# VectorE's row products put into loops with register addresses, in a BatchNorm convolution gate over two images

## The reference, cut to what matters

```python
xg  = group_norm(x, 32 groups)                       # no affine
y1  = bn_relu(sum over h of xg[b,c,h,:] * w1[c,h])   # (b, c, 256)
y2  = bn_relu(sum over w of xg[b,c,:,w] * w2[c,w])   # (b, c, 256)
dot = sum over k of y1[b,c,k] * y2[b,c,k]
p   = softmax over c of ((dot @ lw1.T + lb1) @ lw2.T + lb2)
out = x + xg * p[b,c]
```

## Time and profile before

| What | Value |
|---|---|
| Median of three runs | 1724.97 us |
| The profiled execution, its own time | 1723.45 us |
| Its span on the core | 1721.1 us |
| DMA, moved over the span | 724.02 MB, mean 421 GB/s |
| VectorE busy | 928.2 us, 54% |
| ScalarE busy | 664.3 us, 39% |
| TensorE busy (matmuls) | 561.4 us, 33% |
| GpSimd busy | 336.8 us, 20% |
| VectorE's row products (L920) | 1856, busy 643.1 us, with 155.0 us of accumulator reads |

### The profile page before, as it was taken

One profiled execution on the slowest core, in us unless ns is written; L12 is line 12 of the kernel. 1 busy time (PEld: TensorE's weight loads), 2 busy tenths in 40 slices (PEclk: granted clock), 3 DMA queues, 4 the chain that ended last, 5 costly groups with the idle time before them and its releaser, 6 DMA issues.

```text
span 1721.1 us, 14879 instructions
## 1 busy us (share of the span) xinstructions
PE 561.4 (33%) x4326; PEld 229.5 (13%) x4326; DVE 928.2 (54%) x4104; ACT 664.3 (39%) x507; POOL 336.8 (20%) x475
## 2 busy tenths in 40 slices
PE   4588766554334433433354344430000000000000
PEld 1123212122111211111121122110000000000000
DVE  5899999957455655555566547772222222222220
ACT  4687987856344455444555446610000000000000
POOL 7678888820000000000000000000000000000000
PEclk8799888876565655656556555765555555555555
DMA  9999999989999999999999999989999999999999
GB/s 394 425 427 426 415 396 425 429 342 419 430 429 429 431 430 430 429 431 429 430 430 430 401 429 430 401 331 431 433 432 428 431 433 432 432 429 431 433 432 404
DMA packets 52146, 724.02 MB, mean 421 GB/s; under 512 B 6241, under 2 KB 6753, under 8 KB 8034
## 3 DMA queue, kind: packets, MB, share of 16 engines
q1 hardware_dynamic: 33922, 458.84, 62.9%
q10 hardware_dynamic: 18144, 264.25, 36.1%
HBM read 454.63 MB, written 268.44 MB: 420 GB/s over the span
## 4 chain that ended last, share of the span: by engine, by line
DMA 51%; another core or an unknown queue 27%; DVE 7%; PE 6%; ACT 3%; issue 2%; SPq 1%; POOL 0%; ACTq 0%; DVEq 0%; POOLq 0%
DMA xs<-in_x 44%; DMA out<-xs 6%; DVE mul_junk L920 5%; PE ps_part L521 2%; ACT sq_junk L733 2%; DVE xs L994 2%; DMA xs<-in_w 1%; SPq L344 1%; ACT xs L800 1%; PE ps_part L651 1%; PE ps_part L536 1%; PE ps_y L549 1%; PE ps_l L613 0%; PE ps_l L622 0%
## 5 line engine op out<-in xcount | busy, mean ns | idle before, releaser
L920 DVE SCALAR_TENSOR_TENSOR mul_junk<-xs,ps_w 128x256 fp8e5<-128x256 f32 x1856 | 643.1, 418 | 291.4 <-DMA xs<-in_x 288.7
L733 ACT ACTIVATE sq_junk<-xs 128x4096 fp8e5<-128x4096 f32 x128 | 463.3, 3619 | 284.5 <-DMA xs<-in_x 276.1
L994 DVE TENSOR_SCALAR xs<-xs,scale,shift 128x4096 f32<-128x4096 f32 x95 | 227.1, 2412 | 392.0 <-DMA xs<-in_x 391.4
L536 PE MATMUL ps_part<-xs,taps 128*32 128x256 f32 x2048 | 221.7, 609 | 414.4 <-DMA xs<-in_x 414.4
L521 PE MATMUL ps_part<-xs,taps 128*32 128x512 f32 x1024 | 157.8, 764 | 104.5 <-DMA xs<-in_x 99.8
L800 ACT ACTIVATE xs<-xs,shift,scale 128x4096 f32<-128x4096 f32 x33 | 125.4, 3801 | 112.2 <-DMA xs<-in_x 107.9
L536 PEld LDWEIGHTS ps_part<-xs,taps 128*32 128x32 f32 x2048 | 92.9, 163 | 522.7 <-issue 350.1
L434 POOL TENSOR_TENSOR rstd_b<-var,minus_half 128x1 f32<-128x1 f32 (+1 forms) x36 | 20.5, 568 | 708.7 <-DVE var L944 708.7
L920 DVE DVE_READ_ACCUMULATOR mul_junk<-xs,ps_w 128x1 f32 x1856 | 155.0, 83 | 0.0
L405 POOL TENSOR_TENSOR xs<-xs 128x768 f32<-128x768 f32 x64 | 116.4, 1824 | 59.6 <-DMA xs<-in_x 56.8
L521 PEld LDWEIGHTS ps_part<-xs,taps 128*32 128x32 f32 x1024 | 44.2, 135 | 208.2 <-issue 208.2
(11 more groups left out here) (108 smaller groups left out, 348.2 us busy)
## 6 DMA issues: line engine op xcount, KB each, us to landing
xs<-in_x SPq DMA_DIRECT2D x214, 2048.0 KB, 27.6
out<-xs ACTq DMA_DIRECT2D x126, 2048.0 KB, 33.3
xs<-in_lw SPq DMA_DIRECT2D x2, 2048.0 KB, 16.0
out<-xs SPq DMA_DIRECT2D x2, 2048.0 KB, 11.1
w_c<-in_w_rows SPq DMA_DIRECT2D x1, 512.0 KB, 3.8
w_sb<-in_w SPq DMA_DIRECT2D x1, 512.0 KB, 9.0
xs<-in_w SPq DMA_DIRECT2D x1, 512.0 KB, 23.2
xs<-in_g SPq DMA_DIRECT2D x2, 16.0 KB
```

The lines of the kernel that those rows point to most:

```text
L536: last = nc.tensor.matmul(ps_part[b][32 * a:32 * a + 32, 0:W], taps[:, g % 2, hf * JH + j, :], xs[:, s, j * W:(j + 1) * W], start=(hf == 0 ...
L733: nc.scalar.activation(sq_junk[:], xs[:, s, :], ACT.Square, accum_out=sq_sum[:, u % 2, u // 2, b:b + 1], saturate=False).then_inc(squared, 1)
L920: last = nc.vector.scalar_tensor_tensor(out=mul_junk[:, sets[0] % 2, j - first, :], in0=xs[:, s, j * W:(j + 1) * W], scalar=1.0, saturate= ...
L994: return nc.vector.tensor_scalar(xs[:, s, :], xs[:, s, :], scale[:, b, g:g + 1], shift[:, b, g:g + 1], ALU.mult, ALU.add)
```

## The change

`multiply_rows` no longer writes its rows out: each half-unit's sets become a loop on VectorE, whose counter gives the addresses of the row in `xs`, of the column in `y2s` and, in the first stage, of the scratch row. The loop's counter also gives the value that `rows_done` must have.

In the first stage the loop runs over three sets, and the thirteenth row stands behind it. Each of the 13 rows has a scratch row of its own (`early_junk`, uint8, in the part of slot 9 that the first stage uses for small things); a set waits for the same set of the half-unit before. In the second stage the loop runs over four sets, all write to the same four rows of `mul_junk` (now bf16, without a second buffer), and each set waits for the one right before it. `rows_done` starts at `SETS` instead of 0, and the waits on it on SyncE and TensorE are raised by as much.

```diff
+def rows_before(u, b):
+    return SETS * (position(u, b) + 1)
...
+        early_junk = early(DVE_ROWS * W // 4).bitcast(mybir.dt.uint8).rearrange("p (r w) -> p r w", r=DVE_ROWS)
...
-        mul_junk = sb("mul_junk", [P, 2, SET, W], mybir.dt.float8e5)
+        mul_junk = sb("mul_junk", [P, SET, W], bf16)
...
-                sp.wait_ge(rows_done, SETS * (position(u, b) + 1))
+                sp.wait_ge(rows_done, rows_before(u, b) + SETS)
...
-                    pe.wait_ge(rows_done, SETS * 4 * (g - 1))
+                    pe.wait_ge(rows_done, SETS * (4 * (g - 1) + 1))
...
-                    pe.wait_ge(rows_done, SETS * 4 * QG * (q + 1))
+                    pe.wait_ge(rows_done, SETS * (4 * QG * (q + 1) + 1))
...
-                rows = DVE_ROWS if u < FIRST else JH
-                for first in range(0, rows, SET):
-                    if sets[0] >= 2:
-                        dve.wait_ge(rows_done, sets[0] - 1)
-                    for j in range(first, min(first + SET, rows)):
-                        row = (u % 2) * JH + j
-                        last = nc.vector.scalar_tensor_tensor(
-                            out=mul_junk[:, sets[0] % 2, j - first, :], in0=xs[:, s, j * W:(j + 1) * W], scalar=1.0, saturate=False,
-                            in1=ps_w2[g % 2][:, 0:W], op0=ALU.mult, op1=ALU.mult,
-                            accum_out=y2s[:, g % (2 * QG), b, row:row + 1])
-                    last.then_inc(rows_done, 1)
-                    sets[0] += 1
+                before = rows_before(u, b)
+
+                def row(out, j):
+                    return nc.vector.scalar_tensor_tensor(
+                        out=out, in0=xs[:, s, bass.ds(j * W, W)], scalar=1.0, in1=ps_w2[g % 2][:, 0:W],
+                        op0=ALU.mult, op1=ALU.mult, accum_out=y2s[:, g % (2 * QG), b, bass.ds(j + (u % 2) * JH, 1)])
+
+                if u < FIRST:
+                    with dve.Fori(0, SETS - 1) as i:
+                        dve.wait_ge(rows_done, i + (before - SETS + 1))
+                        for j in range(SET):
+                            last = row(early_junk[:, bass.ds(i * SET + j, 1), :], i * SET + j)
+                        last.then_inc(rows_done, 1)
+                    dve.wait_ge(rows_done, before)
+                    row(early_junk[:, DVE_ROWS - 1, :], DVE_ROWS - 1).then_inc(rows_done, 1)
+                else:
+                    with dve.Fori(0, SETS) as i:
+                        dve.wait_ge(rows_done, i + before)
+                        for j in range(SET):
+                            last = row(mul_junk[:, j, :], i * SET + j)
+                        last.then_inc(rows_done, 1)
...
+            dve.sem_inc(rows_done, SETS)
             for u in range(FIRST):
```

More of the change, by code:

```diff
@@ L900, in setup @@
                     ).then_inc(masks_summed, 1)
-            sets = [0]
             def multiply_rows(u, b):
```

## The result

The changed kernel takes 1717.3 us (median of 6 runs, 1715.6 to 1720.0) beside 1723.92 us for the kernel before (6 runs, 1722.68 to 1725.1): ratio 0.9961, 95% interval 0.995 to 0.9973. The profiled execution took 1720.0 us, its span is 1717.8 us.

What follows compares the result with a forecast made beforehand. The prediction took the kernel to be bound by its transfers. Its terms, 0 + 1.9 - 0.4 = +1.5 us on 1724.97 us, gave 1726.5 us, with a range of 1720 to 1762 us.

Steps and rivals of the forecast that it cites:

- (7): Instruction queues: if half of the 0.38 MB on VectorE's queue goes, 0.19 MB fewer bytes at 421 GB/s, -0.4 us.
- Rival C: Instruction fetches, all stages: they cost more than their bytes, so less code saves up to 4.9 us, 1721 us; chance 0.15.
- (1): Shifted `rows_done` values on SyncE and TensorE, and new scratch types: same moments, elements and passes, 0 us.
- (2): First-stage wait: the same set of the half-unit before is long finished, so no drain, 0 us.
- (3): First-stage instructions around VectorE's rows: seven address, wait, counter and branch instructions, 0.2 to 0.56 us a set, hidden.
- 280 us, 0.34 apart: Sign of being right, first stage: VectorE busy near 280 us of 304, row products still 0.34 us apart.
- rival A: First stage: VectorE's sequencer sets the pace if each row computes its own addresses; +21 us, 1746 us; chance 0.20.
- (4): Second-stage wait: each set drains VectorE, 0.25 us a set (0.11 to 0.43), 64 us in all, covered by idle time.
- my upper price: VectorE's sequencer: a register or branch instruction costs at most 0.08 us.
- (5): End of second stage: twelve drained sets add 3.0 us, less 1.1 us of VectorE's waiting: +1.9 us (0.2 to 4.1).
- (6): End of first stage: VectorE waited 2.81 us for TensorE there, so 0 us.
- Rival B: Loops across instruction packet edges: code is fetched again at each turn back, about +15 us, 1740 us; chance 0.15.

Runs made afterwards that it cites:

- vector_code16: The kernel after with 16 already-met waits on VectorE ahead of every second-stage half-unit's loop: 1721.79 us, ratio 0.9978 to the kernel before.
- one_turn2: The kernel after with each second-stage loop of four turns written as four loops of one turn: 1727.52 us, ratio 1.0016 to the kernel before.
- sync_code64: The kernel after with 64 already-met waits on SyncE ahead of every ordinary second-stage load: 1728.65 us, ratio 1.0016 to the kernel before.
- first_only: The kernel after with second-stage rows written out again with two buffers, loops in the first stage only: 1723.43 us, ratio 0.9996 to the kernel before.
- second_only: The kernel after with first-stage rows written out, keeping its scratch rows and waits, loops in the second stage only: 1717.4 us, ratio 0.9964 to the kernel before.
- drain_unrolled: The kernel before with one second-stage buffer, each set waiting for the set just before, no loops: 1725.57 us, ratio 0.9997 to the kernel before.
- second_tail: The kernel after with first-stage rows and the last channel group's second-stage half-units written out: 1720.01 us, ratio 0.9967 to the kernel before.
- sync_code16: The kernel after with 16 already-met waits on SyncE ahead of every ordinary second-stage load: 1717.71 us, ratio 0.9959 to the kernel before.

## Why the prediction was wrong

The step that failed is **(7) "Less code"**, priced by bytes at -0.4 us. The queue lost 8 of its 46 packets, 0.07 MB, and the kernel 6.6 to 7.0 us; vector_code16 put 4 packets and half of that time back, with no other change than the waits themselves. Two things were missing. A fetch holds up one share of a load for longer than its record lasts (1.0 us against 0.3, below), and a load lands with its last share, so that the engines' reads and the rotation of slots go by it. And this adds up: over 520 us at 430 GB/s, from 445 to 965 us, the last share fell behind by 23.3 us before and 15.9 to 19.6 after. That more code to fetch makes it worse is shown by vector_code16, one_turn2 and sync_code64; why a fetch costs that much is not, nor how much of the growth would be there without any.

**Rival C** named the cause (fetches cost more than their bytes) and gave 1721 us at 0.15. It took its price from the wrong sign: GB/s that rise from 425 towards 431. They did not, in either stage: 421 GB/s after and 420 before in the first, 427 and 428 in the second. The lateness shows in GB/s only where slots run out of loads in flight, near 965 us and at the stages' ends. It also put the larger part of the effect (304 x 11/431 = 7.8 of 12.3 us) in the first stage; by first_only and second_only it is all in the second, and what the first stage's end gained in a profile, the second began with as a later last share (7.1 us in first_only and 8.3 in the kernel after, 1.9 in the kernel before). That its 1721 us lies near the measured 1717.3 is in part luck: the rates that its 4.9 us were made from did not change.

Step by step. (1) 0 us for values and types: a product still takes 0.42 us, right. (2) and (3), the first stage: the row's pace did exceed what I allowed in part of the sets (VectorE 286.0 us busy instead of 280.6, SyncE waiting 20.2 us for it), but nothing was lost, as first_only shows with 0.9996; right in the result, and the stated sign "280 us, 0.34 apart" wrong (0.34 to 0.61 us over most turns). The reason given was wrong too: the trace records two address steps for each row, 0.09 and 0.05 us, so each row does compute its own addresses, which was rival A's condition. Its price was what failed: those steps run beside the row before, and a half-unit grew by 0.22 us and not by 0.35. Rival A did not come about, by 0.05 us a half-unit. (4) I took 0.25 us a set for the drain; it is 0.35 us at the turn and 0.04 us behind the first row, of which the drain is 0.12. Of the rest the branch may be the larger part: its record lasts 0.06 us, but the next register step or wait starts 0.19 us after the branch's start where the loop turns back (192 times in the second stage, median) and 0.10 us where it doesn't; my upper price was 0.08. It is covered, as said: drain_unrolled 0.9997. (5) +1.9 us at the end of the second stage: the two pairs of profiles differ there by 2.3 and 0.8 us, but no run shows it in the time. (6) I gave 0 us to the end of the first stage, and the single pair of profiles seemed to give 5.7 us there; first_only and the repeated profile show no lasting gain: right in the time. (7) is the step above. Rival B (edges of code blocks) did not appear: no gap of microseconds between turns, 38 packets instead of more.

## What to carry to other kernels

In a kernel bound by transfers, count the instruction packets beside its loads: here 8 packets of 8 KB fewer came with 6.6 us, and 15 more with some 10 us lost (of it up to 2.5 us by the added waits themselves), though the whole queue is 0.1% of the transfers. A wait that is met adds code like any instruction, and time where loads are issued one after the other. Loops can pay by that even on an engine whose rows they slow down, as long as it has idle time. And compare a kernel with its own second profile before a place is named: two executions of the kernel before differed by 22 GB/s in the very slice that seemed to explain the gain.

## What the runs showed of the hardware that I had not expected

The late share: near 965 us the last of a load's 16 steps came 25.2 us behind the fourth in the kernel before, the one before it 13.5 us, and the other fourteen within 6.1 us. One or two shares carry it. From 445 to 965 us the two latest shares together fell behind by a further 33.5 us in the kernel after (mean of its two profiles, 35.4 and 31.6; 10 packets in the second queue in that time), 36.1 us in the kernel before (35.3 and 36.9; 14 packets), 43.3 us in one_turn2 (17) and 47.1 us in sync_code64 (20). That is 0.7, 1.4 and 1.4 us for each further packet, while the record of such a packet lasts 0.31 us. It is a size and no constant: two profiles of one kernel differ by 4 us, and with 10 packets second_only has 30.4 us and second_tail 37.5, with 12 vector_code16 41.1 and with 13 sync_code16 37.1.

In the first stage single steps can be seen. From 50 to 340 us the loads land 4.9 us apart, but now and then 5.4 to 6.1 us, mostly 5.9, and from then on the last share is 0.5 to 1.2 us later, mostly 1.0. Each of the six profiles with straight rows in the first stage has 13 such steps, each of the eight with loops has 10. For 156 of these 158 steps a packet of the second queue (8 KB) lies between the two landings or up to 2 us ahead of them, for the 625 landings without a step in 125 cases; the 16 KB packets of the first queue, 34 in every profile, which I take for TensorE's, lie there by themselves 2 times, and by themselves between landings without a step 5 to 12 times in each profile. So the packets that hold up the last share are those of the second queue, and the 3 steps fewer are what the loops save in the first stage, where they bought no time.

Which share a fetch falls on isn't shown by any record, and it seems to decide: the same engine's code was free at 4 packets and dear at 15, and in the kernel after, repeated, the two latest shares are almost even (17.7 and 17.2 us), where in the kernel before one is nearly twice as late as the other (25.2 and 13.5); but in the kernel after's first profile they are not (27.9 and 17.3). Part of the gain may be this distribution and not the number. So may be the sudden rise of vector_code16, whose last share grew as in straight code (23.9 us) on 2 packets more up to 965 us. A shift of the code without a change of its length would tell; it wasn't tried. Nor was a TensorE with shorter code; the first stage gives no sign that it would help.
